# Contexts loaded into the spare weights buffers of the last expert tiles, and two context products moved between the early mixes

## The reference, cut to what matters

```python
x = x + _L0_attn_ref(_layernorm(x), ...)
x = x + _L0_xattn_ref(ctx_1024, _layernorm(x), mask, ...)
x = x + _L0_ffn_ref(_layernorm(x), ...)     # 8 experts, one per row, then a layernorm
x = x + _L1_attn_ref(_layernorm(x), ...)
x = x + _L1_xattn_ref(_layernorm(x), ctx_1024, ctx_1024, mask4, 0, ...)
x = x + _L1_ffn_ref(_layernorm(x), ...)
```

```python
score = jnp.einsum('bhqd,bhkd->bhqk', Q, K) / dk
ctx = jnp.einsum('bhqk,bhkd->bhqd', jnp.where(mask, -jnp.inf, score), V)
```

## Time and profile before

| | us |
|---|---|
| median of 3 runs | 1706.41 |
| the runs | 1706.38, 1706.41, 1715.8 |
| the profiled execution | 1714.85 |
| its span in the profile | 1713.0 |
| TensorE busy | 1622.8 (95%) |
| DVE / ACT / GpSimd busy | 1100.7 / 800.7 / 552.0 |

### The profile page before, as it was taken

How to read it: one execution, slowest core, us unless ns; L and a number is a source line. 1 busy time by engine, 2 the same in 40 slices (tenths; PEclk the granted TensorE clock), 3 DMA queues, 4 the chain that set the end, 5 groups by cost and what they waited for, 6 DMA issues and landing times. The chain is left out here.

```text
span 1713.0 us, 33366 instructions
## 1 busy us (share of the span) xinstructions
PE 1622.8 (95%) x11462; PEld 1309.2 (76%) x11462; DVE 1100.7 (64%) x2578; ACT 800.7 (47%) x2227; POOL 552.0 (32%) x589
## 2 busy tenths in 40 slices
PE   6999899999999999999999998899988999987998
PEld 5877678787878878778878777799967867765775
DVE  5466467666676666676766664456445388848796
ACT  2255344554544544545445441355412467753442
POOL 1022223333333333333333343335350033345200
PEclk9999999999999999999999998899999999999998
DMA  3100210000000000000001004486330000010000
GB/s 103 41 18 1 92 37 11 11 10 7 3 10 10 10 10 10 0 10 10 10 10 41 24 2 145 117 257 201 109 97 21 1 26 1 1 61 1 1 22 22
DMA packets 48808, 67.45 MB, mean 39 GB/s; under 512 B 11826, under 2 KB 42770, under 8 KB 46034
## 3 DMA queue, kind: packets, MB, share of 16 engines
q1 hardware_dynamic: 47186, 62.66, 11.8%
q0 software_dynamic: 1536, 3.67, 0.7%
HBM read 57.02 MB, written 9.31 MB: 39 GB/s over the span
## 5 line engine op out<-in xcount | busy, mean ns | idle before, releaser
L709 POOL TENSOR_TENSOR l0x_p<-l0x_p,l0x_inv 112x488 f32<-112x488 f32 x256 | 261.9, 1044 | 424.1 <-DVE l0x_inv L806 422.9
L934 ACT ACTIVATE l0x_p<-l0x_s,l0x_low 112x488 f32<-112x488 f32 x256 | 177.9, 696 | 254.6 <-DVE l0x_low L795 225.9
L795 DVE CUSTOM_DVE_ANT_0 l0x_s<-l0x_score_ps,l0x_bias 112x488 f32<-112x488 f32 x256 | 160.2, 663 | 94.5 <-PE l0x_score_ps L1081 85.7
L1089 PEld LDWEIGHTS l0x_pT_ps<-ident,l0x_p 112*122 112x122 f32 x1024 | 99.0, 138 | 45.5 <-issue 39.0
L1102 PE MATMUL l0x_oT_ps<-l0x_pT,l0x_v 122*64 122x112 f32 x2048 | 127.2, 266 | 7.0 <-ACT l0x_pT L940 6.1
L1102 PEld LDWEIGHTS l0x_oT_ps<-l0x_pT,l0x_v 122*64 122x64 f32 x2048 | 99.6, 137 | 42.6 <-issue 32.0
L1089 PE MATMUL l0x_pT_ps<-ident,l0x_p 112*122 112x112 f32 x1024 | 126.6, 266 | 0.7 <-POOL l0x_p L709 0.6
L782 DVE TENSOR_TENSOR l0x_kT_lo<-l0x_proj_ps,l0x_kT_hi 128x488 fp32r<-128x488 f32 x128 | 84.2, 667 | 62.0 <-ACT l0x_kT_hi L924 62.0
L1037 PE MATMUL l0x_proj_ps<-l0x_kvT_hi,l0x_wkv_hi 128*128 128x488 f32 x256 | 104.5, 408 | 2.9 <-DVE l0x_kvT_lo L770 2.9
L1046 PE MATMUL l0x_proj_ps<-l0x_wkv_hi,l0x_kvT_hi 128*122 128x512 f32 x256 | 104.9, 410 | 0.0
L1048 PE MATMUL l0x_proj_ps<-l0x_wkv_hi,l0x_kvT_lo 128*122 128x512 f32 x256 | 100.9, 394 | 0.0
(11 more groups left out here) (402 smaller groups left out, 4121.4 us busy)
## 6 DMA issues: line engine op xcount, KB each, us to landing
l0f_w<-in_l0f_w SPq DMA_DIRECT2D x21, 1024.0 KB
l0x_c_in<-in_ctx SPq DMA_DIRECT2D x16, 375.0 KB
l1x_gram_context<-in_ctx SPq DMA_DIRECT2D x16, 375.0 KB
sorted_x<-l0x_zeros SPq DMA_DIRECT2D x1, 2816.0 KB, 15.6
l0f_xs<-sorted_x SPq DMA_DIRECT2D x21, 128.0 KB, 2.1
sorted_y<-l0f_z SPq DMA_DIRECT2D x21, 128.0 KB, 1.7
l0x_wkv<-in_l0x_wkv SPq DMA_DIRECT2D x2, 1024.0 KB, 9.5
x<-in_x SPq DMA_DIRECT2D x4, 448.0 KB, 8.3
```

Source lines behind the costliest of these rows:

```text
L709: nc.gpsimd.tensor_tensor(p[:, i % 2, a, :], p[:, i % 2, a, :], inv[:, i % 2, a:a + 1].broadcast_to([S, KEYS]), ALU.mult).then_inc(pn_read ...
L795: nc.vector.tensor_tensor_reduce(s_sb[:, h % 2, :], score_ps[0:S, h % 2, 0:KEYS], bias[:], -SCALE, 3.4e38, ALU.add, ALU.min, low[:, h:h + ...
L934: nc.scalar.activation(p[:, h // 2 % 2, h % 2, :], s_sb[:, h % 2, :], ACT.Exp, scale=-1.0, bias=low[:, h:h + 1], accum_out=total[:, h:h + ...
L1089: done = nc.tensor.transpose(pT_ps[0:KT, a, t * S:(t + 1) * S], p[:, i % 2, a, t * KT:(t + 1) * KT], ident[0:S, 0:S])
```

## The change

- `AHEAD = 2`: the products of contexts 6 and 7 are made in `make_mixes(0)`, behind the fourth and the fifth gram product. SP loads them with contexts 4 and 5, ACT copies them before the tiles. `gram` keeps its ten slots: n % 10.
- Contexts 8 and 9 are loaded in tiles 7 and 9 into the context buffer, the mask in tile 11 and its four reductions follow tiles 15 to 18.
- Contexts 10 to 15 (`SPARE`) are loaded into `w1`, two in the buffer of each of tiles 18, 19 and 20, once that tile's expansion is done. DVE writes their columns of ones with six small memsets.
- The eight products left after the tiles read the context buffer for 8 and 9 and `w1` for 10 to 15.
- `norm(0)` of `l1_attention` is made in `l0_experts`: DVE waits for `rstd_step` 8 behind the first late `take_gram_k`, and then makes one of the eight normalisations behind each `take_mix`.

```diff
-    EARLY = 6
+    EARLY, AHEAD = 6, 2
+    SPARE = EARLY + 4
+    QB = 4
...
         def gram_slot(n):
-            return n if first(n) else n - EARLY
+            return n % GN
+
+        def spare_tile(n):
+            return TILES - 3 + (n - SPARE) // 2
+
+        def spare_rows(n):
+            at = (n - SPARE) % 2 * F
+            flat = w1[0:CT, spare_tile(n) % 3].rearrange("p c f -> p (c f)")
+            return flat[:, at:at + NC * (D + 1)].rearrange("p (t d) -> p t d", d=D + 1)
+
+        def context_rows(n):
+            return context[:, n % 4] if n < SPARE else spare_rows(n)
...
         def _(sp):
-            for n in range(4, EARLY):
+            for n in range(4, EARLY + AHEAD):
                 load_context(n)
...
-                if i == 1:
-                    sp.dma_start(masked[:], A["score_mask"].rearrange("b s n -> s b n")).then_inc(mask_w, 16)
-                if i < 4:
-                    load_context(EARLY + i)
-                elif i == 4:
+                if i == 4:
                     for part, source in next_w.loads(A):
                         sp.dma_start(part, source).then_inc(next_w_w, 16)
+                elif i in (7, 9):
+                    load_context(EARLY + AHEAD + (i - 7) // 2)
+                elif i == 11:
+                    sp.dma_start(masked[:], A["score_mask"].rearrange("b s n -> s b n")).then_inc(mask_w, 16)
+                elif i >= TILES - 3:
+                    sp.wait_ge(hT_done, 2 * i + 2)
+                    for n in range(SPARE, B):
+                        if spare_tile(n) == i:
+                            sp.dma_start(spare_rows(n)[:, :, 0:D], A["ctx"][n].rearrange("(c p) d -> p c d", p=CT)
+                                         ).then_inc(spare_w[i % 3], 16)
                 if i >= 1:
                     store_tile(i - 1)
             store_tile(TILES - 1)
-            for n in range(EARLY + 4, B):
-                load_context(n)
...
         def _(dve):
+                if i >= TILES - 3:
+                    dve.wait_ge(hT_done, 2 * i + 2)
+                    for n in range(SPARE, B):
+                        if spare_tile(n) == i:
+                            nc.vector.memset(spare_rows(n)[:, :, D:D + 1], 1.0).then_inc(spare_ones, 1)
                 residual(i)
                 normalise(i)
-                if 4 <= i < 8:
-                    find_masked(i - 4)
+                if 15 <= i < 19:
+                    find_masked(i - 15)
...
+            def normalise_first(j):
+                row = j % QB
+                scale = (rstd2, rstd)[j // QB]
+                nc.vector.tensor_scalar(first_rows[:, (1 - j // QB) * QB + row, :], x[:, row, :], mv[:, row, 0:1],
+                                        scale[:, row:row + 1], ALU.subtract, ALU.mult)
             take_key_sums(1)
             take_gram_k(EARLY)
+            dve.wait_ge(rstd_step, 8)
             for n in range(EARLY + 1, B):
                 take_gram_k(n)
                 take_mix(n - 1)
+                if n - EARLY - 1 < 2 * QB:
+                    normalise_first(n - EARLY - 1)
...
         def _(pe):
             def multiply_context(n, parts):
-                    if n == EARLY:
+                    if n < SPARE:
+                        since(pe, context_w[n % 4], 16 * (n // 4))
+                    else:
+                        pe.wait_ge(spare_w[spare_tile(n) % 3], 32)
+                        pe.wait_ge(spare_ones, n - SPARE + 1)
+                    if n == EARLY + AHEAD:
                         pe.wait_ge(gelu_ready, 2 * TILES)
...
                 for n in range(begin + 1, end):
                     multiply_gram(n)
+                    if g == 0 and 3 <= n < 3 + AHEAD:
+                        multiply_context(EARLY + n - 3, (0, 1))
                     multiply_mix(n - 1)
...
-            for n in range(EARLY, B):
+            for n in range(EARLY + AHEAD, B):
                 multiply_context(n, (0, 1))
...
# l1_attention
                 def norm(q):
-                    if q >= 1:
-                        dve.wait_ge(inT_done, q * 2)
+                    dve.wait_ge(inT_done, q * 2)
...
-                norm(0)
                 for q in range(Q):
```

More of the change, by code:

```diff
@@ L1241, in l0_experts @@
         z_var, z_rstd = ph.sb("z_var", [128, 2]), ph.sb("z_rstd", [128, 2])
-        y = x1
+        y = first_rows = x1
         context, wk, wv = gram_in.context, gram_in.wk, gram_in.wv
@@ L1275, in l0_experts @@
         context_w = [ph.sem("context_w0"), ph.sem("context_w1"), ph.sem("context_w2"), ph.sem("context_w3")]
+        spare_w = [ph.sem("spare_w0"), ph.sem("spare_w1"), ph.sem("spare_w2")]
+        spare_ones = ph.sem("spare_ones")
         gram_done, gram_ready = ph.sem("gram_done"), ph.sem("gram_ready")
@@ L1586, in take_gram @@
                 act.wait_ge(gram_done, n + 1)
-                if not first(n):
+                if n >= GN:
                     act.wait_ge(gram_k_ready, EARLY)
@@ L1618, in activate @@
                                          ).then_inc(hT_hi_ready, 1)
-            for n in range(EARLY):
+            for n in range(EARLY + AHEAD):
                 take_gram(n)
@@ L1637, in multiply_context @@
                 if parts[0] == 0:
-                    since(pe, context_w[n % 4], 16 * (n // 4))
-                    if n == EARLY:
+                    if n < SPARE:
[4 more added lines that the diff above has]
+                    if n == EARLY + AHEAD:
                         pe.wait_ge(gelu_ready, 2 * TILES)
@@ L1643, in multiply_context @@
                     for t in range(NC):
-                        done = nc.tensor.matmul(hT_ps[:, 2 * (n % 2) + c, 0:D + 1], context[:, n % 4, t, c * 128:(c + 1) * 128],
-                                                context[:, n % 4, t, :], start=(t == 0), stop=(t == NC - 1))
+                        done = nc.tensor.matmul(hT_ps[:, 2 * (n % 2) + c, 0:D + 1],
+                                                context_rows(n)[:, t, c * 128:(c + 1) * 128],
+                                                context_rows(n)[:, t, :], start=(t == 0), stop=(t == NC - 1))
                 if parts[-1] == KC - 1:
@@ L1751, in _ @@
             transpose_tile(1)
-            pe.wait_ge(gram_ready, EARLY)
+            pe.wait_ge(gram_ready, EARLY + AHEAD)
             pe.wait_ge(gram_k_ready, EARLY)
@@ L1974, in transpose_inputs @@
                 def transpose_inputs(q, n):
-                    pe.wait_ge(norm_ready, q * 2 * QB + (n + 1) * QB)
                     if q >= 1:
+                        pe.wait_ge(norm_ready, (q - 1) * 2 * QB + (n + 1) * QB)
                         pe.wait_ge(act_step, in_step(q - 1, 0 if n == 0 else 2))
```

## The result

The changed kernel takes **1692.12 us** (median of four executions, 1690.92 to 1694.17) against 1708.63 us for the kernel before, measured beside it: ratio 0.990, 95% interval 0.9878 to 0.9922. On another chip it was 1693.23 us (seven executions), 13.8 us under the median of the kernel before there; two of the seven took 8 and 9 us more than their own median, and the ratio that counts them is 0.9931 (0.9906 to 0.9955), 12 us. Together that is 12 to 17 us less, where I forecast 6.6 us less and 1699.8 us. It is rival (a), 12.6 us less and 1693.8 us, that came; the result lies at the lower edge of my range, 1692 to 1707.

A forecast was written before the change was run, and what follows sets the result against it. TensorE was taken to set the pace, losing time to late loads and, next, to DVE behind GpSimd's gathers. Early products 0.5, late part 4.7 and next block 1.4 gave 6.6 us off 1706.41: 1699.8 us, range 1692 to 1707.

The forecast's parts named there:

- rival (a): Tile loop: the common execution has the tile stall too, so all 12.6 us count, giving 1693.8 us; chance 20%.
- the choice of the stall that the common execution lacks: Tile loop: the 6.0 us stall was assumed chance, absent from the common execution, so its gain was not counted.
- Early tiles: Tiles 0 to 3: moving four context loads and the mask away removes the late tile rows, gaining 6.0 us.
- Early products: Early mixes: products of contexts 6 and 7 fit into TensorE's waits for DVE; +0.5 us, ends -5.3 and +1.0.
- Rival (b): Early mixes: DVE's halt is absent or elsewhere, so the early products cost TensorE 5.3 us, giving 1705.6 us; chance 10%.
- Last tiles: Late products to first mix: spare-buffer loads start mixes 7.5 us earlier, less 2.8 us of slow clock, net +4.7.
- DVE's added work: Late mixes: eight normalisations of 0.35 us fit DVE's 0.66 us idle per period, so cost 0; uncovered, 2.8 us.
- start of the next block: Next block's head: TensorE's transposes start when the barrier opens instead of after DVE's normalisations, gaining 1.4 us.
- Rival (c): Tile 11: the mask alone, with 376-byte rows, holds SP and the stall only moves, giving 1705.8 us; chance 10%.
- Rival (d): Tiles 18 to 20: stores queue behind six context loads and delay the gathers, 34 us late, 1734; chance 4%.

The follow-up runs named there:

- e1: The kernel before, unchanged, in another execution: 1707.22 us (12 executions); its profiled execution took 1704.49 us.
- e4: The kernel before with only contexts 10 to 15 moved into the weights buffers of the last three tiles: 1697.78 us, ratio 0.994.
- e7: The kernel before with only the first eight normalisations moved into the late mixes: 1703.51 us, ratio 0.9982.
- e3: The kernel before with only the products of contexts 6 and 7 moved between the early mixes, contexts 8 and 9 loaded in tiles 0 and 1: 1704.91 us, ratio 0.9983.
- e2: The kernel before with only tile-loop loads moved: contexts 6 to 9 to tiles 5, 7, 9, 13, the mask to tile 11: 1700.79 us, ratio 0.9957.
- e6: The kernel before with only contexts 6 to 9 moved, to tiles 5, 7, 9 and 13, the mask left in tile 1: 1701.40 us, ratio 0.9972.
- e5: The kernel before with only the mask load moved, from tile 1 to tile 11, contexts left in tiles 0 to 3: 1704.22 us, ratio 0.9988.
- e10: The changed kernel with key sums and first gram taken by DVE ahead of the last gathered group: 1691.21 us, ratio 0.991 to the kernel before.
- e11: As e10, but the last group done row by row between the mixes, deviations wait and normalisations after the sixth: 1686.29 us, ratio 0.9881 to the kernel before.
- e8: The changed kernel without its two early products, contexts 6 to 9 loaded in tiles 5, 7, 9 and 13: 1691.03 us, ratio 0.9909 to the kernel before.
- e12: As e11, without the two early products, contexts 6 to 9 in tiles 5, 7, 9 and 13: 1689.68 us, ratio 0.99 to the kernel before.

## Why the prediction was wrong

- **The step that failed is the choice of the stall that the common execution lacks.** "I assume the common execution has no such stall and differs by 2.4 us elsewhere" set the 6.0 us of the tile loads to nothing. e1, e4 and e7, with the tile loads left in place, and e3, with the mask and two of the four contexts, show the stall with the same long issue (6.3 to 6.7 us); e2 takes it away and is 4.5 us shorter in the tiles. What the profiled execution had more than e1, 10.3 us, was to 5.6 us DVE's pauses: its early part is 62.56 us, those of the other traces 55.97 to 58.00. With that turned round the sum is rival (a)'s: 12.6 us in all, 1693.8 us. That the time came within 1.7 us of this is in part luck: the kernel before measured 1708.63 us beside it, 2.2 us above the 1706.41 that I started from, and the terms below err in both directions.
- **Early tiles, 6.0 us:** right in place, 5.0 us against e1 and 6.1 against the profiled execution. It takes the contexts to cause it (e6), as I read from the earlier trace rows, and the mask adds to it (e5).
- **Early products, +0.5 us:** the net is nothing within the scatter (56.47 against 55.97 to 56.96), which is near my term, but the cover was wrong. I named DVE's halts; it is the wait of 4.54 us for tile 0's rows, which the profiled execution hid behind those halts, and the clock of the first expansion behind it (3.80 us in place of 4.7 to 5.9). That the size came near is luck. Rival (b) had the condition right, the halts were absent, and its price wrong for the same reason. In e10 and e11 the clock did not come back, and the early part was 1.5 us longer than in the changed kernel.
- **Last tiles, 7.5 us less 2.8 of clock:** the first mix came 8.5 us earlier than in e1 and the half clock cost 2.0, so 6.5 net for my 4.7. The shape was as forecast: products in 21 us, one wait of 5.24 us, clock 0.50. The mis-sized terms: the clock cost 2.0 in place of 2.8; counted from the first late product the gathers were issued 0.5 us later than I took, landed 0.4 us sooner (1.7 for my 2.1), and from there to the first mix it was 3.9 us for my 4.5; and e1's first mix comes 0.5 us later than the one I reckoned from.
- **DVE's added work, 0, and start of the next block, 1.4 us:** both as forecast (e7: 22.09 and 1.44 us).
- **Rival (c)**, the mask alone in tile 11 as a stall: no row of the changed kernel shows a wait there, and e6 has the mask in its old tile without one. In e5, with the mask alone moved to tile 11, the store behind it stands 3.24 us in its issue and no rows are late for it. The rule that I weighed for it, the Trainium skill's (DMA: Bandwidth & Descriptors, "Specifications") on pieces under 512 bytes, does not decide here: the mask's issue takes 0.43 us in e6 and TensorE waits for nothing behind it.
- **Rival (d)**, stores behind the spare loads, is there in small: the first gather starts 5.55 to 5.57 us after the first late product in all seven traces without these loads, and 5.91 to 6.42 in all seven with them, e4 among them, and the last gather ends 0.5 to 1.3 us later (26.1 to 26.6 against 25.3 to 25.6). That is on the path to the first mix of the changed kernel. My sign for (d), 6 us, lies inside that spread. The landing pays it back: the last group is there 1.7 us behind the last gather, where it took 4.5 to 4.7 without the spare loads. Whether the gathers start later because the last stores are issued behind the loads, or because they share the DMA engines, is not separated.
- The stages from e1 to the changed kernel add to 0.5 + 5.0 + 6.5 + 1.4 = 13.4 us; the medians of the two comparisons say 16.5 and 13.8. What each part gives alone by its ratio (tile loads 7, early products 3, spare buffers 10, normalisations 3 us) adds to more than that, but each has an interval of 3 us either way, so that the early products and the normalisations alone are not told from nothing, and the two gains in the late part do not add: the spare buffers alone make it 8.1 us shorter than e1, with two products fewer it is 6.5.

## What to carry to other kernels

One profiled execution that is 8 us above the median has something that the common one lacks, and which of its stalls that is can't be argued from how much like chance it looks; a cause that stands in the program (a fixed order of loads on one queue) speaks for the common case, and a halt that nothing in the program explains speaks for chance. Give both the weight of a case, or look at a second execution first. Work moved ahead of a wait gives nothing until the next bound is moved too: the two early products were worth -1 to -2 us behind DVE's old order and 3 to 4.5 us behind the new one, and an engine that reaches a wait earlier may pay for it in clock. And where a short dependent result stands in a queue behind a batch that waits for a DMA, take it first and spread the batch.

## What the runs showed of the hardware

- DVE's halts of 4.62 and 6.90 us were in one trace of fourteen, which also has one of ACT under the late products (10.27 us before 1261.23, released by nothing that the profile shows, like the longer one of DVE). The 3.03 us of TensorE in the earlier trace rows fall into ACT's; it cost nothing, since e1, which waits for context loads there instead (0.8 to 2.0 us four times), takes 40.25 us against 40.00. Of 72 timed executions of the kernel before, beside the experiments, seven took over 1713.8 us, with a mean granted clock of 0.972 to 0.976 where the others had 0.979 to 0.986; two of eleven of the changed kernel were likewise 8 to 10 us above its median, at 0.976. So the change does not remove them. That these executions have such halts is a guess, since none of them was traced, and the traced execution with the halts had a clock of 0.978, between the two groups. What causes the halts stays open.
- The clock after a wait is not the same each time. Behind 5.24 us (changed kernel, first mix) and 2.95 us (e10, second mix) a mix took 2.07 us, half clock; behind 3.03 us in the earlier trace rows a product ran at full clock. The same first expansion of the tiles took 3.80 us in the changed kernel and 5.44 in e11, with 0.9 us of wait ahead of both: 1.6 us that no edit explains. The granted clock of 1083 to 1087 us is 1.00 in the one and 0.58 in the other.
- With one context load per tile in tiles 0 to 3, SP stands up to 4.3 us in the issue of the stores behind them (e5), and with the mask too 6.7 us in the issue of a context (e1). Spread over tiles 5 to 13 the context loads are issued in 0.36 to 0.74 us each (e2, e6, e8, e12; 0.37 us in the changed kernel).
